# Two transformer blocks on one Trainium2 core: 22 of 32 input tiles transposed on VectorE in 32x32 squares, and two activation buffers that change roles

## The reference

```python
# block 1 (16 heads of 32; _sln: layer norm, then gamma * ln + beta, per sequence from cond)
h   = _sln(hidden, w, ...)
q, k, v = split(h @ Wqkv.T + bqkv)
att = softmax(q @ k.T) / D ** 0.5
h1  = (att @ v) @ Wp.T + bp + hidden
x   = _sln(h1, w, ...) + h1
# block 2 (one head; film: x * (1 + scale) + shift, per sequence from cond)
h = film(rmsnorm(x, norm1_w), cond, film1_w, film1_b)
x = x + softmax((h @ q_w + q_b) @ (h @ k_w + k_b).T * D ** -0.5) @ (h @ v_w + v_b) @ proj_w + proj_b
h = film(rmsnorm(x, norm2_w), cond, film2_w, film2_b)
x = x + gelu(h @ mlp_w1 + mlp_b1) @ mlp_w2 + mlp_b2
```

## Time and profile before

| | |
|---|---|
| median of 3 runs | 1479.72 us (1478.57 to 1479.89) |
| the profiled execution, its own time | 1478.36 us |
| its span, first to last instruction | 1476.5 us |
| TensorE busy | 1467.3 us (99%) |
| VectorE, ScalarE, GpSimd busy | 935.3, 669.8, 621.9 us |
| granted clock of TensorE | full, in every slice |
| main loop of the first block | about 49 to 552 us |

### The profile page before, as it was taken

How to read it: one execution, slowest core, us unless ns; L and a number is a source line. 1 busy time by engine, 2 the same in 40 slices (tenths; PEclk the granted TensorE clock), 3 DMA queues, 4 the chain that set the end, 5 groups by cost and what they waited for, 6 DMA issues and landing times.

```text
span 1476.5 us, 24231 instructions
## 1 busy us (share of the span) xinstructions
PE 1467.3 (99%) x8714; PEld 1194.1 (81%) x8714; DVE 935.3 (63%) x1878; ACT 669.8 (45%) x2024; POOL 621.9 (42%) x544
## 2 busy tenths in 40 slices
PE   8999999999999999999999999999999999999999
PEld 5888888888888668888888788888888888888887
DVE  6677777777776676887767644763458434763354
ACT  4656556555553454656665433332324323332210
POOL 5756666766654556766846102401123102401001
PEclk9999999999999999999999999999999999999999
DMA  7222232232213534797544855545454545545342
GB/s 259 69 76 98 72 105 75 80 101 73 76 69 122 199 144 131 258 326 262 189 170 151 313 206 192 158 157 214 164 193 141 193 186 179 163 159 216 132 137 92
DMA packets 92792, 232.58 MB, mean 158 GB/s; under 512 B 9664, under 2 KB 17856, under 8 KB 87552
## 3 DMA queue, kind: packets, MB, share of 16 engines
q1 hardware_dynamic: 90848, 216.24, 42.5%
q10 hardware_dynamic: 1824, 14.79, 2.4%
HBM read 174.17 MB, written 56.82 MB: 156 GB/s over the span
## 4 chain that ended last, share of the span: by engine, by line
PE 97%; DVE 1%; POOL 1%; issue 0%; ACT 0%; POOLq 0%
PE bank L728 20%; PE bank L730 20%; PE bank L729 20%; PE bank L1234 7%; PE bank L1238 7%; PE bank L1236 7%; PE bank L819 4%; PE bank L812 2%; PE bank L830 2%; PE bank L1156 2%; PE bank L1051 1%; PE bank L869 1%; PE bank L861 1%; PE bank L743 1%; PE bank L1187 1%; POOL xa L2296 1%
## 5 line engine op out<-in xcount | busy, mean ns | idle before, releaser
L1343 ACT ACTIVATE pa<-bank,neg_max 128x128 f32<-128x128 f32 x512 | 181.2, 407 | 133.7 <-DVE neg_max L1753 133.7
L728 PE MATMUL bank<-w_hi,g_hi 128*128 128x512 f32 x512 | 200.6, 392 | 0.0
L730 PE MATMUL bank<-w_hi,g_lo 128*128 128x512 f32 x512 | 199.4, 390 | 0.0
L729 PE MATMUL bank<-w_lo,g_hi 128*128 128x512 f32 x512 | 199.4, 390 | 0.0
L1234 PE MATMUL bank<-op_hi,ring 128*128 128x512 f32 x448 | 174.9, 390 | 0.6 <-DVE op_lo L1658 0.3
L1238 PE MATMUL bank<-op_hi,ring 128*128 128x512 f32 x448 | 174.5, 390 | 0.0
L1236 PE MATMUL bank<-op_lo,ring 128*128 128x512 f32 x448 | 174.5, 389 | 0.0
L2341 POOL TENSOR_TENSOR pa<-pa,rec 128x512 f32<-128x512 f32 x128 | 142.9, 1125 | 52.3 <-DVE rec L1776 52.2
L2313 POOL TENSOR_TENSOR xrc<-xrc,b 128x512 f32<-128x512 f32 x32 | 49.7, 1585 | 269.1 <-DMA xrc<-x_dram 269.1
L1606 ACT ACTIVATE sum<-sum,cols 128x512 f32<-128x512 f32 x128 | 92.0, 722 | 114.0 <-DVE sum L2179 113.9
L1343 ACT ACTIVATION_READ_ACCUMULATOR pa<-bank,neg_max 128x1 f32 x512 | 126.5, 247 | 0.0
(11 more groups left out here) (266 smaller groups left out, 3541.0 us busy)
## 6 DMA issues: line engine op xcount, KB each, us to landing
ring<-w_dram SPq DMA_DIRECT2D x32, 1792.0 KB, 7.5
rows<-st_dram SPq DMA_DIRECT2D x32, 512.0 KB, 4.2
hid_dram<-sum SPq DMA_DIRECT2D x64, 256.0 KB, 2.2
hid<-hid_dram SPq DMA_DIRECT2D x64, 256.0 KB, 2.7
w_dram<-w_parts ACTq DMA_DIRECT2D x8, 1792.0 KB, 6.1
xa<-xt_in SPq DMA_DIRECT2D x32, 256.0 KB, 4.1
xra<-xt_in SPq DMA_DIRECT2D x32, 256.0 KB, 2.8
x_dram<-h SPq DMA_DIRECT2D x32, 256.0 KB, 2.0
```

Of the source, the lines that this page charges most:

```text
L728: nc.tensor.matmul(dst, w_hi, a_hi, start=start, stop=False)
L729: nc.tensor.matmul(dst, w_hi, a_lo, start=False, stop=False)
L730: return nc.tensor.matmul(dst, w_lo, a_hi, start=False, stop=stop)
L1343: last = nc.scalar.activation(pa[:, j, m, :], scores_bank[j][:, m * P:(m + 1) * P], ACT.Exp, bias=neg_max[:, j * C + m:j * C + m + 1], acc ...
```

## The change

Tiles 0 to 9 go as before. For tiles 10 to 31 (TURN = 10):

- Each tile is loaded twice. SyncE loads it plainly for the statistics alone (`load_stat`, into `xa[:, 2 + n % 2]`). ScalarE's queue loads it a second time in squares (`load_squares`, four DMAs of 32 partitions into `xa[:, n % 2]`): partition 32q + j gets, for chunk c and square w, the 32 features from c * 128 + 32q of token 32w + j. So the squares lie where they belong in the transposed tile, and only the inside of each 32x32 square is still to be transposed. Each contiguous run is 128 bytes, 512 of them per DMA.
- The mean and deviation of a token must now reach lanes of other partitions. GpSimd writes them into two masked rows of 128x4 (`stats_a`, `stat_rows`), TensorE multiplies these by a constant 128x128 matrix (`same_lane`, one where two partitions agree modulo 32) into `x_bank` (`spread_stats`, after `attend(t)`), and VectorE copies the 128x8 result to `stat_lanes` (`copy_stats`, at the end of its step).
- GpSimd normalizes the squares in place, four instructions of 128x4x32, at the start of the next step, ahead of `add_bias` and `scale_p` (`norm_squares`).
- VectorE transposes all squares with one instruction into `hf` (`turn`, between the copy of the queries and `add_x1`). `scale_a` reads `hf` instead of `x_bank`, and waits for `x_turned`.
- VectorE makes the two constants before the loop (`make_squares`), and at t = 0 takes the statistics of tiles 9 and 10.

In the second block `hb_new` and `hb` become `hb[0]` and `hb[1]`, used in turn by group; the eight copies and their semaphore are gone.

The diff, its core (left out: the renaming of `hb_new` and `hb` at their uses, and the counts that semaphores reused later start from):

```diff
@@ -20,6 +20,8 @@
 AHEAD = 2 * GB
+TURN = AHEAD + 2
+SQ = 32
@@ -208,8 +214,7 @@
         wvp_lo = run("wvp_lo", [P, C, D], F32R)
-        hb_new = run("hb_new", [P, C, GT])
-        hb = run("hb", [P, C, GT])
+        hb = [run("hb0", [P, C, GT]), run("hb1", [P, C, GT])]
@@ -417,6 +427,10 @@
+        def squares_in(n):
+            return 16 * (3 + GB * ((n - TURN) // 2 + 1))
@@ -429,6 +443,14 @@
                 sp.dma_start(xa[:, n % GB], tokens(xt, n)).then_inc(x_in[n % GB], 16)
+            def load_stat(n):
+                if n < TURN + 2:
+                    sp.wait_ge(n_done, n - GB + 1)
+                else:
+                    sp.wait_ge(bn_done, n - 1)
+                sp.dma_start(xa[:, 2 + n % 2], tokens(xt, n)).then_inc(x_in[2 + n % 2], 16)
@@ -474,16 +496,17 @@
             sp.wait_ge(st_stored, 16)
-            for n in range(2 * GB, 3 * GB - 1):
+            for n in range(2 * GB, TURN):
                 load_x(n)
+            load_stat(TURN)
...
                     load_rows(t - 1)
-                if t + 3 * GB - 1 < NB:
-                    load_x(t + 3 * GB - 1)
+                if t + TURN + 1 < NB:
+                    load_stat(t + TURN + 1)
@@ -743,6 +766,16 @@
+            def spread_stats(n):
+                pe.wait_ge(rstd_ready, n + 1)
+                if n == TURN:
+                    pe.wait_ge(n_scaled_act, TURN - 2)
+                else:
+                    pe.wait_ge(n_scaled_dve, n - TURN + 2)
+                nc.tensor.matmul(x_bank[:, 0:2 * P // SQ], same_lane[:], stat_rows[:, n % 2], start=True, stop=True)\
+                    .then_inc(n_done, 1)
@@ -993,12 +1026,12 @@
                     transpose_p(t, j)
-                if t + AHEAD < NB:
+                if t + AHEAD < TURN:
...
                 if b == 0 and not ahead:
-                    pe.wait_ge(n_scaled_act, NB - 2)
+                    pe.wait_ge(n_scaled_dve, NB - TURN + 2)
@@ -1026,6 +1059,8 @@
                 attend(t)
+                if t > 0 and t + AHEAD + 1 < NB:
+                    spread_stats(t + AHEAD + 1)
@@ -1307,11 +1340,26 @@
+            def load_squares(n):
+                if n < TURN + 2:
+                    act.wait_ge(n_done, n - 1)
+                else:
+                    act.wait_ge(x_turned, n - TURN - 1)
+                src = tokens(xt, n).rearrange("(w j) (c q i) -> q j c w i", j=SQ, c=C, i=SQ)
+                for q in range(P // SQ):
+                    nc.scalar.dma_start(xa[q * SQ:(q + 1) * SQ, n % 2].rearrange("j (c w i) -> j c w i", c=C, i=SQ), src[q])\
+                        .then_inc(x_in[n % 2], 16)
...
-                if n >= GB:
-                    act.wait_ge(lo_ready, n - 1)
-                act.wait_ge(n_done, n + 1)
+                if n >= TURN:
+                    act.wait_ge(x_turned, n - TURN + 1)
+                    src = h_full(n).rearrange("p c t -> p (c t)")
+                else:
+                    if n >= GB:
+                        act.wait_ge(lo_ready, n - 1)
+                    act.wait_ge(n_done, n + 1)
@@ -1419,31 +1467,33 @@
                     round_a(t + AHEAD)
+                if t + TURN < NB:
+                    load_squares(t + TURN)
...
                 act.wait_ge(nb_full, GB * (g + 1) + b + 1)
-                affine(src, hb_new[:, :, b * P:(b + 1) * P], cur_st[:, b], nb_free_act)
...
@@ -1509,7 +1559,6 @@
                 act.wait_ge(blo, GB * g + GB)
-                nc.scalar.activation(hb[:], hb_new[:], ACT.Identity).then_inc(hb_copied, 1)
@@ -1664,12 +1712,38 @@
-                dve.wait_ge(x_in[n % GB], loaded(n // GB + 1))
-                wait(dve, xn_ready, n - 1)
+                if n < TURN:
+                    dve.wait_ge(x_in[n % GB], loaded(n // GB + 1))
+                    src = xa[:, n % GB]
+                else:
+                    dve.wait_ge(x_in[2 + n % 2], loaded(3 + (n - TURN) // 2))
+                    src = xa[:, 2 + n % 2]
+                wait(dve, rstd_ready if n >= TURN + 2 else xn_ready, n - 1)
                 wait(dve, var_ready, 2 * n)
-                nc.vector.bn_stats(stats[:], xa[:, n % GB]).then_inc(bn_done, 1)
+                nc.vector.bn_stats(stats[:], src).then_inc(bn_done, 1)
+            def make_squares():
+                dve.wait_ge(consts_made, 3)
+                then(nc.vector.tensor_reduce(same_lane[:, 0:SQ], ident[:].rearrange("p (w i) -> p i w", i=SQ), AX.X, ALU.add))
+                nc.vector.tensor_copy(same_lane[:, SQ:P].rearrange("p (w i) -> p w i", i=SQ),
+                                      same_lane[:, 0:SQ].unsqueeze(1).broadcast_to([P, P // SQ - 1, SQ]))
+                then(nc.vector.tensor_reduce(in_square[:], ident[:].rearrange("p (w i) -> p w i", i=SQ), AX.X, ALU.add))
+            def copy_stats(n):
+                dve.wait_ge(n_done, n + 1)
+                if n >= TURN + 2:
+                    dve.wait_ge(xn_ready, n - 1)
+                nc.vector.tensor_copy(stat_lanes[:, n % 2], x_bank[:, 0:2 * P // SQ]).then_inc(n_scaled_dve, 1)
+            def turn(n):
+                dve.wait_ge(xn_ready, n + 1)
+                dve.wait_ge(lo_ready, n - 1)
+                nc.vector.transpose(h_full(n).rearrange("p c t -> p (c t)"), xa[:, n % 2]).then_inc(x_turned, 1)
@@ -1869,6 +1943,7 @@
+            make_squares()
@@ -1887,16 +1962,20 @@
                 recip(t, 2)
-                if t + AHEAD + 1 < NB:
-                    var_a(t + AHEAD + 1)
+                if t == 0:
+                    var_a(TURN - 1)
+                    mean_var(TURN - 1)
+                    add_eps(TURN - 1)
+                if t + TURN < NB:
+                    var_a(t + TURN)
...
                     var_2(t - 2)
-                if t + AHEAD + 1 < NB:
-                    mean_var(t + AHEAD + 1)
+                if t + TURN < NB:
+                    mean_var(t + TURN)
...
                     mean_var2(t - 2)
-                if t + AHEAD + 1 < NB:
-                    add_eps(t + AHEAD + 1)
+                if t + TURN < NB:
+                    add_eps(t + TURN)
@@ -1925,10 +2004,14 @@
                     film_table(1, st_f1, x_bank)
+                if TURN <= t + AHEAD < NB:
+                    turn(t + AHEAD)
...
                     residual(t - 1)
+                if t > 0 and t + AHEAD + 1 < NB:
+                    copy_stats(t + AHEAD + 1)
@@ -2286,6 +2369,37 @@
+            pool_steps = [0]
+            def then(instruction):
+                pool_steps[0] += 1
+                instruction.then_inc(pool_step, 1)
+                pool.wait_ge(pool_step, pool_steps[0])
+            def stats_a(n):
+                i = n % 2
+                pool.wait_ge(var_ready, 2 * n + 2)
+                then(nc.gpsimd.tensor_tensor(rstd1[:, i:i + 1], ve1[:, i:i + 1], neg_half[:, 0:1], ALU.pow))
+                if n >= TURN + 2:
+                    pool.wait_ge(n_done, n - 1)
+                w = P // SQ
+                nc.gpsimd.tensor_scalar(stat_rows[:, i, 0:w], in_square[:], mv1[:, i, 0:1], None, ALU.mult)
+                nc.gpsimd.tensor_scalar(stat_rows[:, i, w:2 * w], in_square[:], rstd1[:, i:i + 1], None, ALU.mult)\
+                    .then_inc(rstd_ready, 1)
+            def norm_squares(n):
+                i, w = n % 2, P // SQ
+                pool.wait_ge(n_scaled_dve, n - TURN + 3)
+                pool.wait_ge(x_in[i], squares_in(n))
+                tile = xa[:, i].rearrange("p (c w i) -> p c w i", c=C, i=SQ)
+                for k in range(w):
+                    last = nc.gpsimd.tensor_scalar(tile[:, :, k], tile[:, :, k], stat_lanes[:, i, k:k + 1],
+                                                   stat_lanes[:, i, w + k:w + k + 1], ALU.subtract, ALU.mult)
+                last.then_inc(xn_ready, 1)
@@ -2343,6 +2457,8 @@
             for t in range(NB):
+                if TURN <= t + AHEAD < NB:
+                    norm_squares(t + AHEAD)
@@ -2351,8 +2467,10 @@
                     shift(t - 2)
-                if t + AHEAD + 1 < NB:
-                    norm_a(t + AHEAD + 1)
+                if t == 0:
+                    norm_a(TURN - 1)
+                if t + TURN < NB:
+                    stats_a(t + TURN)
```

54 lines of the change are left out of this document (27 added, 27 removed).

## The result

The changed kernel takes 1488.3 us (median of 4 runs, 1487.33 to 1489.89), the kernel before 1479.2 us (1478.57 to 1479.89, 4 runs): a ratio of 1.0062, 95% interval 1.0045 to 1.008. It is slower by 9 us. The prediction said 1474.4 us with a range up to 1482; it was wrong in sign and in range.

What follows compares the result with a forecast made beforehand. TensorE, busy 1467.3 of 1476.5 us, was taken as the bound. Terms -10.3 + 4.8 + 0.2 = -5.3 us gave 1473.1 from the profiled 1478.4, or 1474.4 us from the median 1479.7; range 1471.5 to 1482.

Steps and rivals of the forecast that it cites:

- Four: 2.0 us (1.9 to 2.1): ScalarE, end of step: four DMA issues of squares take 2.0 us, started about 233.3, done at 235.3.
- 0.85 us late: ScalarE's exponentials: lateness TensorE would not feel, some 0.3 us before VectorE's rec plus 0.55 at TensorE; 0.3 us late was expected.
- The price of lateness: TensorE, per step: a stall lengthens the period and takes half of itself back, so half of lateness beyond 0.85 us shows.
- ScalarE late in every step: Rival, four issues ahead of the next exponentials: about 1507 us at 1.4 us an issue, about 1490 at 1.0; chance 0.09.
- Removal: TensorE, first block: 22 sets of four xa transposes removed at 0.47 us each, -10.3 us.
- Spread product: TensorE, between attend and next scores: 22 fp32 products of same_lane with stat_rows at 0.22 us, +4.8 us (3.1 to 8.6).
- Start of the loop: VectorE at loop start: make_squares and a second set of statistics at t = 0 add 0.2 us (0 to 1).
- Second block: ScalarE: eight copies of hb fall away; TensorE has no wait there, so 0 us.
- Stall: TensorE, first-block loop: ScalarE 0.3 us late does not reach it, so none; 2 us in all if the transposition takes 1.4.
- The rival of a late GpSimd: Rival: pieces of 1.3 us delay the fourth scaling 0.7 us past the slack, about +10 us; decides from 1.05 a piece; chance 0.08.
- The rival by a rule: Rival: short-run loads at 19 times cond's 3.1 us, 59 us per tile, delay norm_squares and TensorE; over 900 us more; chance 0.01.
- next case: ScalarE's four issues: the late-ScalarE rival decides beyond 2.6 us for the four, that is beyond 0.85 us of lateness.

Runs made afterwards that it cites:

- e8: Changed kernel with three of ScalarE's four loads of squares per tile (time only): 1477.1 us, ratio 0.9988 to the kernel before.
- e1: Changed kernel with the loads of the squares issued by SyncE instead of ScalarE: 1474.05 us, ratio 0.9971 to the kernel before.
- e7: Changed kernel with VectorE's copy of the next tile's values ahead of the reciprocals of heads 4 to 7: 1487.67 us, ratio 1.0056 to the kernel before.
- e6: Kernel before with only the second block's part of the change (hb in two buffers, eight copies gone): 1478.81 us against 1478.89.
- e4: Changed kernel with GpSimd normalizing one of the four pieces of a tile (time only): 1488.99 us, ratio 1.007 to the kernel before.
- e11: Changed kernel with VectorE's transposition right behind its last reciprocals, ScalarE's issues left in place: 1474.86 us, ratio 0.9972 to the kernel before.
- e5: Changed kernel with ScalarE's four issues moved behind the key copy, same queue: 1473.93 us, ratio 0.9968 to the kernel before.

## Why the prediction was wrong

**The failed step: "Four: 2.0 us (1.9 to 2.1)".** I priced ScalarE's issues from the load of cond, 0.47 us, and from SyncE's row of four, 2.08 us. Measured, an issue took 0.66 us in the median, so that four take at least 2.65 us, and in 13 of the 22 steps one or two of the four were held up, which made 2.9 to 3.74 us. The bounds of 1.9 to 2.1 were far too narrow for two rows, one of a single transfer (over 128 partitions, the new ones fill 32) and one of another shape on another queue, and the earlier trace rows had the warning: one of 32 plain tile loads took 1.4 us to issue. I used it for the rival alone, and gave that 0.09. The trace of before holds more of it: between 109.94 and 186.97 us six of SyncE's issues took over 1 us, three of tiles and three of rows.

**The slack behind it was too large.** I had the issues start 0.27 us behind the next scores (233.3 against 217.78 + 15.25 = 233.03); in e8 it is 0.22, so this part was right. But I let ScalarE be 0.85 us late, the sum of two slacks, 0.3 and 0.55, which puts the point of decision at 2.6 us for the four. The runs put it at 2.03 us: with 0.22 ahead and 0.10 behind, the exponentials may start 2.35 us after the scores, 0.38 later than the 1.97 of before. That is less than either the sum or the 0.55 at TensorE alone.

The 0.3 did not exist. I read it at the fourth reciprocals (226.28). But the third ones start as soon as the third group of exponentials is done, and VectorE's whole row up to the fourth stands behind them. In the step that I chose, t = 11, this is hidden: h_lo took 1.79 us there (220.23; GpSimd's add_bias had started 0.06 ahead of it), where it took 0.68 in every other step of the loop. The other 21 steps of t = 2 to 23 of the kernel before show VectorE waiting for that group, as here t = 12:

```profile
240.06 0.18 DVE L1776 RECIPROCAL rec<-sums 128x4 f32<-128x4 f32 x1 [0.51 <-ACT pa L1343]
```

So lateness passes almost whole: in e1 the fourth scaling starts 8.78 us behind the scores (118.01), in the changed kernel at t = 17, whose exponentials are 0.83 us late, 9.58 (330.32). What is left is the slack at TensorE, 0.55 by the rows of before and 0.38 by the runs.

Another place that I had not looked at is the copy of the values: it is queued behind the reciprocals of the second group of exponentials, and TensorE waited for it up to 1.2 us. Step by step against e1, it takes part only where the exponentials are 0.85 us late or more; below that, and so in nearly all late steps, the stall is at pa alone. With the copy moved (e7) the late periods average 15.62 us instead of 15.64, and the wait shows at pa.

**The price of lateness was right below 2.93 us and wrong above.** The rival took half of (lateness - slack) per step, "a stall lengthens the period and so takes half of itself back". That is what the late steps show. But with four issues of 3.6 us it gives (3.6 - 2.03) / 2 = 0.8 us, and the loop 12.84 + 3.6 - 15.32 = 1.1, which is what was measured. The rival's 1490 us came near the measured 1488.3 by luck: its four issues of 1.0 us were too long (3.05 us for the four on average), its slack too large and its price too low. The rival "ScalarE late in every step" is what happened, at its place and with its sign.

**The sum, term by term.** Without the stall the change is worth 419.28 - 415.31 = 4.0 us up to t = 24 (e1 against before), where 5.3 was predicted. Of it:
- Removal: right, -10.3 us. A step with neither transposes nor product takes 15.00 to 15.03 us, as at t = 24 before.
- Spread product: predicted 0.22 (0.14 to 0.39), measured 15.32 - 15.03 = 0.29, so 6.4 us instead of 4.8; with 15.00, the step of t = 23, it would be 0.32. Mis-sized inside its bounds; its 1.6 us, less the 0.2 of the next term, are the 1.3 that are missing. What it waits for is early, as said: no wait of TensorE names it in the changed kernel.
- Start of the loop: predicted 0.2. The scores of t = 0 start between 49.11 and 50.06 us in the kernels here, at 49.40 before; nothing to be told from no effect.
- Second block: predicted 0, measured 0 (e6).
- Stall: predicted 0, measured 13.9, and 0.27 of later start. -10.3 + 6.4 + 13.9 + 0.3 = +10.3; 429.46 - 419.28 is 10.18.

**GpSimd.** Right, and no part of the loss (e4). (The rival of a late GpSimd was mis-added: with pieces of 1.3 us the scaling ends 10.2 - 8.74 - 0.55 = 0.9 us past the slack, not 0.7; no piece came near.) A piece was taken at 0.70 us with bounds of 0.52 and 0.89; the rows are 797 ns, inside the bounds, 3.42 us for four:

```profile
L2399 POOL TENSOR_SCALAR xa<-xa,stat_lanes x88: 790/797/1086, 80.0 to 417.2; 128x128 f32<-128x128 f32 x88
...
L2389 POOL TENSOR_SCALAR stat_rows<-in_square,rstd x22: 292/811/827, 63.7 to 397.0; 128x4 f32<-128x4 f32 x22
```

The median of the second row, 0.81 us for 128x4, is not its price: in e1 each of the 22 took 0.29 or 0.30. In the changed kernel 13 took 0.81 to 0.83; each of them started up to 0.03 us ahead of VectorE's add_x1 and ended about 0.1 behind its end (110.16 to 110.97, add_x1 110.17 to 110.88). They stand at the end of GpSimd's step and delay nothing.

**VectorE.** The transposition was taken at 0.7 us between bounds of 0.69 and 1.4; it took 703 to 705 ns in 22 rows:

```profile
L1746 DVE STREAM_TRANSPOSE hf<-xa x22: 703/703/705, 92.8 to 427.6; 128x512 f32<-128x512 f32 x22
```

That is a plain pass over 128x512, as the rows of before suggested. The Trainium skill says of the transposing mode that it is "Pipelined to sustain one element per cycle per lane" ("Vector Engine (DVE) Microarchitecture Reference", 3.8 The reshape front-end and per-opcode configuration); the trace agrees in kind, since the copies and sums of the same size took 0.68 to 0.72 us. That this row fits was right and was the wrong question. It fitted before TensorE's next need, but it stood in the loop, behind 2.48 us of pta copies and the copy of q, and ScalarE waited 4.30 us for it with nothing else to do. With it 3.7 us earlier in the loop the stall is gone (e11).

**DMA and the rule.** Loading each tile twice in short runs disturbed nobody: landing took 2.5 us in the median where the issues stood apart (e5), 4.9 where they met SyncE's, and had 15 us. The rival by a rule did not come; it had multiplied a plain load's landing by 19, while the Trainium skill ("VectorE: DVE Perf Modes", The three transpose paths) states that factor against the DMA's own transposing path. Another rule of the Trainium skill bears on the result: starting DMAs from several engines only saves the sequencer's time to start them, "which is usually small relative to the DMA itself" ("DMA: Bandwidth & Descriptors", Issuing engines are not separate DMA queues). The trace agrees, 0.66 us against 2.5 to 4.9 us to landing; but here the landing had 15 us and the starting had 2.03 us for four, so the small part was the one that counted.

**What would have shown it beforehand.** I followed ScalarE forward through one step and compared its lateness with the slack at TensorE. The path also closes on itself: each part of it waits for the part before, in every step, so its length had to be added up too and set against the period. And with 2.0 us taken for the issues where the limit is 2.03, the forecast stood on the edge; a range whose next case began 0.6 us further on did not say so.
